# Token mixing with one folded product of the query and key weights, and a number per key added in the gating

## What is computed

```python
def token_mixing(x, d_gamma, Wq, bq, Wk, bk, Wv, bv, Wo, bo, a):
    q, k, v = x @ Wq + bq, x @ Wk + bk, x @ Wv + bv
    scores = einsum('btd,bsd->bts', q, k)                 # no softmax
    retained = einsum('bts,bsd->btd', d_gamma * scores, v)
    y = retained @ Wo + bo
    return where(y >= 0, y, a * y)
h = token_mixing(x, ...)
h = h + attn(layernorm(h))      # encoder and decoder LSTMs, 1024 steps each
h = h + ffn(layernorm(h))       # 8 experts, 2 chosen per token
```

## Time and profile before

| | us |
|---|---|
| median of 3 runs | 3925.51 (3924.63 to 3928.59) |
| the profiled execution | 3921.38 |
| its span, first to last instruction | 3919.6 |
| TensorE busy in the span | 3750.3 (96%) |
| VectorE busy | 3139.5 (80%) |
| ScalarE busy | 2391.9 (61%) |
| Pool busy | 85.4 (2%) |
| mean granted TensorE clock | 0.986 |

### The profile page before, as it was taken

How to read it: one execution, slowest core, us unless ns; L and a number is a source line. 1 busy time by engine, 2 the same in 40 slices (tenths; PEclk the granted TensorE clock), 3 DMA queues, 4 the chain that set the end, 5 groups by cost and what they waited for, 6 DMA issues and landing times. The chain is left out here.

```text
span 3919.6 us, 159989 instructions
## 1 busy us (share of the span) xinstructions
PE 3750.3 (96%) x61932; PEld 2749.2 (70%) x61932; DVE 3139.5 (80%) x21227; ACT 2391.9 (61%) x11882; POOL 85.4 (2%) x129
## 2 busy tenths in 40 slices
PE   7899999999999999999999899999999999999998
PEld 3333888888888888888888666666666666666664
DVE  6999899999999999999998677766777667776675
ACT  3232898888889889888887344444444443444443
POOL 6100000000000000000000000000000000000000
PEclk8999999999999999999999999999999999999999
DMA  3111000000000000000000000000000000000000
GB/s 91 22 25 23 3 3 3 3 3 3 3 3 3 3 3 3 3 3 3 3 3 4 4 8 8 8 6 6 8 8 8 6 7 7 8 8 6 6 8 7
DMA packets 49571, 34.01 MB, mean 9 GB/s; under 512 B 37661, under 2 KB 46877, under 8 KB 48806
## 3 DMA queue, kind: packets, MB, share of 16 engines
q1 hardware_dynamic: 48806, 23.77, 2.3%
HBM read 15.37 MB, written 8.39 MB: 6 GB/s over the span
## 5 line engine op out<-in xcount | busy, mean ns | idle before, releaser
L740 PE MATMUL bank<-xs,ident 128*128 128x128 f16 x15583 | 1415.1, 223 | 0.0
L740 PEld LDWEIGHTS bank<-xs,ident 128*128 128x128 f16 x15583 | 1010.2, 102 | 252.2 <-issue 229.8
L760 ACT ACTIVATE ifg_cell_dec<-bank 128x48 f32<-128x48 f32 x1024 | 215.2, 210 | 641.3 <-PE bank L752 641.3
L752 PE MATMUL bank<-enc_lo,u_hi 128*128 128x16 f16 x8192 | 530.1, 173 | 0.3 <-DVE enc_lo L812 0.3
L749 PE MATMUL bank<-enc_hi,u_lo 128*128 128x16 f16 x8192 | 527.8, 173 | 0.0
L775 DVE SCALAR_TENSOR_TENSOR terms_dec<-ifg_cell_dec 128x32 f32<-128x32 f32 x1024 | 197.1, 193 | 398.3 <-ACT ifg_cell_dec L760 387.2
L749 PE MATMUL bank<-enc_hi,u_hi 128*128 128x16 f16 x8192 | 501.6, 170 | 0.0
L749 PEld LDWEIGHTS bank<-enc_hi,u_lo 128*128 128x128 f16 x8192 | 338.4, 96 | 205.6 <-DVE enc_hi L806 171.2
L767 ACT ACTIVATE bank<-twice_cell_dec 128x16 f32<-128x16 f32 x1024 | 191.7, 187 | 402.4 <-DVE twice_cell_dec L781 402.4
L752 PEld LDWEIGHTS bank<-enc_lo,u_hi 128*128 128x128 f16 x8192 | 339.3, 96 | 67.9 <-DVE enc_lo L812 0.4
L749 PE MATMUL bank<-ring_hi,u_lo 128*128 128x16 f16 x4096 | 260.7, 172 | 102.3 <-DVE ring_hi L806 96.0
(11 more groups left out here) (268 smaller groups left out, 7900.8 us busy)
## 6 DMA issues: line engine op xcount, KB each, us to landing
g_rows<-tok_d_gamma_batched_dram SPq DMA_DIRECT2D x8, 512.0 KB, 6.5
x_rows<-in_x_dram SPq DMA_DIRECT2D x16, 256.0 KB, 3.0
kept_h<-tok_ln_h SPq DMA_DIRECT2D x32, 128.0 KB, 2.1
res<-kept_h SPq DMA_DIRECT2D x32, 128.0 KB
out_dram<-sums SPq DMA_DIRECT2D x32, 128.0 KB
raw_wd<-in_L_attn_Wd_dram SPq DMA_DIRECT2D x2, 256.0 KB
raw_experts<-in_L_ffn_W_dram SPq DMA_DIRECT2D x2, 256.0 KB
raw_u<-in_L_attn_Uf_dram SPq DMA_DIRECT2D x1, 256.0 KB
```

The source lines that it names most:

```text
L740: nc.tensor.matmul(spare, m.ident16[:], m.xs[:, 0, :, :].rearrange("p b t -> p (b t)"), start=False, stop=True, skip_group_check=True)
L752: last = nc.tensor.matmul(z[k], m.u_hi[c.d][:, g, :], h_lo, start=False, stop=True, skip_group_check=True)
L760: nc.scalar.activation(c.ifg_cell[:, 0:3, :], ifg, ACT.Tanh, scale=1.0 / Z_SCALE).then_inc(c.s_t_ifg, 1)
```

## The change

The scores of a batch are x M x^T plus terms with one bias, where M = Wq Wk^T. Setup makes M, Wk bq, Wq bk and bq . bk on TensorE and ScalarE. Per batch the kernel computes `k_full` = M' x for 1024 keys (two tiles, no bias matmul; ScalarE adds a bias per partition), splits it into `k_hi` and `k_lo`, and scores are k_hi and k_lo (stationary) times `xT` (moving), which is therefore double-buffered. The part that depends on the key alone comes out of the value matmuls as a 65th column; ScalarE copies it into `d_col`. The gate adds it and multiplies by gamma. The low halves are subtractions in SBUF, on VectorE for batches 0 to 4 (t = 10 and 12), on Pool for batches 5 to 15.

```diff
 # setup, SP
-                for raw, w in zip(raw_qk, (a["L0_tok_Wq"], a["L0_tok_Wk"])):
-                    for k in range(2):
-                        load(raw[k * D:(k + 1) * D, :], w)
+                load(wq[:], a["L0_tok_Wq"])
+                load(wk[:], a["L0_tok_Wk"])
+                load(wq_bq[:, D:DV], a["L0_tok_bq"][:, None])
+                load(bk[:], a["L0_tok_bk"][:, None])
...
-                for k, name in enumerate(("bq", "bq", "bk", "bk")):
-                    load(raw_mix[:, k * D:(k + 1) * D], a["L0_tok_" + name][None, :].broadcast_to([3, D]), s_b, n_b)
 # setup, TensorE (ScalarE copies each result: 4 turned weights, raw_k, two columns, raw_wvo, raw_mix)
-                nc.tensor.transpose(m.bank[4][0:D, 0:D], wv[:], m.ident[0:D, 0:D]).then_inc(s_v, 1)
+                for n, w in enumerate((wv, wq, wk)):
+                    last = nc.tensor.transpose(m.bank[4][0:D, n * D:(n + 1) * D], w[:], m.ident[0:D, 0:D])
+                last.then_inc(s_v, 1)
...
+                mm(m.bank[7][:, 0:DV], wkT[:].rearrange(twice), wq_bq[:], start=True, stop=True)
+                mm(m.bank[7][:, DV:DV + 1], wqT[:].rearrange(twice), bk[:], start=True, stop=True).then_inc(s_v, 1)
...
+        PE_TILE = {7: 0, 9: 1}
+        DVE_TILE = {10: 0, 12: 1}
+        POOL_FROM = 5
...
 # Pool, behind split_weights
+                for b in range(POOL_FROM, B):
+                    for half in range(2):
+                        cols = slice(half * HALF, (half + 1) * HALF)
+                        pool.wait_ge(s_hi, 2 * b + half + 1)
+                        nc.gpsimd.tensor_tensor(k_lo[b % 2][:, cols], k_full[half][:], k_hi[b % 2][:, cols], ALU.subtract
+                                                ).then_inc(s_lo_pool, 1)
 # TensorE, scores
-                    for q, stop in ((q_hi, False), (q_lo, True)):
-                        last = mm(z, k_both[k][:, s * P:(s + 1) * P], q[k][:, half * HALF:(half + 1) * HALF],
+                    for keys, stop in ((k_hi, False), (k_lo, True)):
+                        last = mm(z, keys[k][:, s * P:(s + 1) * P], xT[k][:, half * HALF:(half + 1) * HALF],
                                   start=not stop, stop=stop)
 # TensorE, prep t == 5: two banks, 65 columns
-                            z = bank[6][:, c * D:(c + 1) * D]
+                            z = bank[6 - c // 4][:, c % 4 * DV:(c % 4 + 1) * DV]
 # TensorE, prep, tiles
+                        pe.wait_ge(s_vk, 2 * b + half + 1)
+                        z = bank[6 - half][:]
-                        mm(z, bias, m.ones_s[:], start=True, stop=False)
-                        mm(z, w_hi[:].rearrange("p two d -> p (two d)"), x, start=False, stop=False)
-                        mm(z, w_lo[:].rearrange("p two d -> p (two d)"), x, start=False, stop=True).then_inc(s_tile, 1)
+                        mm(z, m.wk_hi[:].rearrange("p two d -> p (two d)"), x, start=True, stop=False)
+                        mm(z, m.wk_lo[:].rearrange("p two d -> p (two d)"), x, start=False, stop=True).then_inc(s_tile, 1)
 # ScalarE, prep t == 5 and tiles
+                        for half in range(2):
+                            act.wait_ge(s_vo, 2 * b + half + 1)
+                            z = m.bank[6 - half][:, 0:4 * DV].rearrange("p (c d) -> p c d", d=DV)
+                            S.copy(d_col[k][:, 4 * half:4 * half + 4].unsqueeze(2), z[:, :, D:DV])
+                            S.activation(vo[k][:, 4 * half:4 * half + 4, :], z[:, :, 0:D], ACT.Identity,
+                                         scale=MIX_SCALE ** -4).then_inc(s_vk, 1)
...
+                        if b:
+                            wait_low(act, b - 1, half)
+                        z = m.bank[6 - half][:]
+                        S.activation(k_full[half][:], z, ACT.Identity, bias=m.k_col[:, 0:1], scale=1.0 / MIX_SCALE)
+                        S.activation(k_hi[k][:, half * HALF:(half + 1) * HALF], z, ACT.Identity, bias=m.k_col[:, 0:1],
                                      scale=1.0 / MIX_SCALE).then_inc(s_hi, 1)
 # VectorE, gate and low halves
-                    TT(gated[:, n % G_RING, :], m.bank[n % Z_RING][:], m.gT[:, s, half * HALF:(half + 1) * HALF], ALU.mult
-                       ).then_inc(s_g, 1)
+                    STT(gated[:, n % G_RING, :], m.bank[n % Z_RING][:], d_col[b % 2][:, s:s + 1],
+                        m.gT[:, s, half * HALF:(half + 1) * HALF], ALU.add, ALU.mult).then_inc(s_g, 1)
...
-                        STT(low, z, 1.0 / MIX_SCALE, high, ALU.mult, ALU.subtract).then_inc(s_lo, 1)
+                        TT(k_lo[k][:, cols], k_full[half][:], k_hi[k][:, cols], ALU.subtract).then_inc(s_lo, 1)
```

More of the change, by code:

```diff
@@ L38 @@
 BIAS_MIX = 12 * H + D + E
-NBIAS = BIAS_MIX + 5 * D
+DV = D + 1
+NBIAS = BIAS_MIX + DV
 BIG = 2.0 ** 100
@@ L121, in build @@
         m.gate_bias = m.bias[:, 12 * H + D:12 * H + D + E]
-        m.q_bias, m.k_bias = (m.bias[:, BIAS_MIX + k * 2 * D:BIAS_MIX + (k + 1) * 2 * D] for k in range(2))
-        m.vo_bias = m.bias[:, BIAS_MIX + 4 * D:]
+        m.vo_bias = m.bias[:, BIAS_MIX:]
         m.ones3 = sb("ones3", [P, P], BF16)
-        m.ones_s = sb("ones_s", [P, HALF], BF16)
+        m.ones_s = sb("ones_s", [P, P], BF16)
+        m.k_col = sb("k_col", [P, 1], F32)
         m.a_col = sb("a_col", [P, 1], F32)
@@ L167, in setup @@
     with ctx:
[L168 to L171, removed]
+        raw_mix = sb("raw_mix", [3, DV], F32)
+        part = sb("part", [3, 3, DV], BF16)
+        left = sb("left", [3, 3, DV], F32)
+        wq, wk = (sb(n, [D, D], F32) for n in ("wq", "wk"))
+        bk = sb("bk", [D, 1], F32)
+        bk3 = sb("bk3", [D, 3], F32)
+        wqT = sb("wqT", [D, 2, D], F32)
+        wq_bq = sb("wq_turned_bq", [D, DV], F32)
+        wkT = sb("wkT", [D, 2, D], F32)
+        raw_k = sb("raw_k", [P, D], F32)
         wv = sb("wv", [D, D], F32)
@@ L388, in token_mixing @@
         x_split = sb("x_split", [P, NB, 2 * D], F16)
-        xT = sb("xT", [P, T], F16)
-        q_hi = [sb(f"q_hi{k}", [P, T], F16) for k in range(2)]
-        q_lo = [sb(f"q_lo{k}", [P, T], F16) for k in range(2)]
-        k_both = [sb(f"k_both{k}", [P, T], F16) for k in range(2)]
+        xT = [sb(f"xT{k}", [P, T], F16) for k in range(2)]
+        k_hi = [sb(f"k_hi{k}", [P, T], F16) for k in range(2)]
+        k_lo = [sb(f"k_lo{k}", [P, T], F16) for k in range(2)]
+        k_full = [sb(f"k_full{k}", [P, HALF], F32) for k in range(2)]
+        d_col = [sb(f"d_col{k}", [P, NB], F32) for k in range(2)]
         vo = [sb(f"vo{k}", [P, NB, D], F32) for k in range(2)]
@@ L693, in prep @@
                             ).then_inc(s_xs, 1)
-                    if t in DVE_TILE:
-                        n = DVE_TILE[t]
-                        which, half = QK_TILES[n]
+                    if t in DVE_TILE and b < POOL_FROM:
+                        half = DVE_TILE[t]
                         cols = slice(half * HALF, (half + 1) * HALF)
-                        dve.wait_ge(s_hi, 4 * b + n + 1)
-                        if which == "q":
-                            low, high, z = q_lo[k][:, cols], q_hi[k][:, cols], m.bank[5 + n % 2][:]
-                        else:
-                            low = high = k_both[k][D:2 * D, cols]
-                            z = m.bank[5 + n % 2][D:2 * D, :]
-                        STT(low, z, 1.0 / MIX_SCALE, high, ALU.mult, ALU.subtract).then_inc(s_lo, 1)
+                        dve.wait_ge(s_hi, 2 * b + half + 1)
+                        TT(k_lo[k][:, cols], k_full[half][:], k_hi[k][:, cols], ALU.subtract).then_inc(s_lo, 1)
                 for t in range(NT):
```

105 lines of the change are left out of this document (53 added, 52 removed).

## The result

The changed kernel takes 3916.1 us as a median of ten runs (3912.0 to 3919.0). The kernel before, ten runs with the three shown above among them, takes 3926.4 (3919.4 to 3934.7). The ratio is 0.9973, with a 95% interval of 0.9963 to 0.9983, so the change saves 10.3 us, give or take some four. The prediction was 3916.1.

What follows compares the result with a forecast made beforehand. TensorE was taken to bound a steady batch. Setup and the long interval -4.5, one interval -0.5, eleven steady ones -4.9 and the last +0.5 gave -9.4 us: 3912 profiled, 3916.1 us as a median, range 3903 to 3925.

Steps and rivals of the forecast that it cites:

- The floor: TensorE's time for a steady mixing batch: 20.45 less 1.72 us of dropped matmuls, 18.73 us.
- the sum: Total for the mixing: -4.5 to the long interval's end, -0.5, -4.9 in eleven steady intervals, +0.5 at the last; -9.4 us.
- the 1.3 us: TensorE's expected standing time per steady batch, waiting for gates and the LN split, making the period 20.0 us.
- VectorE's own lag: From L644 to the products behind the LN transposes, VectorE alone with eight dearer gates delays TensorE 0.6 us a batch.
- B: Rival: Pool and VectorE miss each other and the number per partition is free; period 18.9, 3903.5 us; chance 0.15.
- C: Rival: gates cost 0.07 more but Pool's work falls beside gates; period 19.3 to 19.4, 3909 us; chance 0.12.
- D: Rival: Pool also holds L682 or L686, or batch 3's k_lo costs another Pool instruction; 3922.5 to 3926.5 us; chance 0.20.
- E: Rival: Pool's subtraction is longer than 1.16 us, each extra microsecond adding one to the period; up to 3938 us; chance 0.06.
- F: Rival: the new gate is streamed at half rate because of its number per partition; 78 us more, 4004 us; chance 0.02.
- SP's last issue ends setup now, so 1.3 us earlier: Setup: without raw_mix loads SP's issues end 1.3 us sooner, so Pool's split and x come 1.3 us earlier.
- my bound: Limit on the change at the long interval's end, taken as -4.5 us with bounds of -1 and -7.
- one instruction further: Case behind the -7 us bound: VectorE is one instruction further when Pool's long instructions end.

Runs made afterwards that it cites:

- e3: Changed kernel, but the gate takes the constant 0.0 instead of the number per key, leaving the key's term out; 3907.4 us.
- e11: Changed kernel with TensorE making the two key tiles at gates 6 and 12 and VectorE's turns at 13 and 15; 3902.0 us.
- e5: Changed kernel with the second key tile made at t = 13 instead of 9 and VectorE's turns at 13 and 15; 3911.0 us.
- e7: Changed kernel with Pool's second subtraction made twice, the first time into a tile nobody reads; 3921.4 us.
- e8: Changed kernel without the two column loads bq and bk, Pool filling their tiles with zeros; 3914.3 us.
- e1: Changed kernel with all low halves of the keys left on VectorE and none on Pool; 3911.2 us.
- e2: Changed kernel with Pool subtracting 8 instead of 512 columns in each half from batch 5 on, all waits kept; 3896.9 us.
- e9: Changed kernel with Pool's bias rows of the later stages made in eight pieces of 201 columns; 3909.4 us.

## Why the prediction was right, and where it was not

**The steady batch: right in its cause and its size.** The floor was 18.73, and 18.78 was measured with both causes out. (A pair of products with its four score matmuls takes 1.98 us, 0.11 more than 1.01 and 4 x 0.215: each pair has a small gap, in both kernels, so the floor holds.) Period 20.0, measured 19.95; the eleven intervals gave -5.2 us for the -4.9 of the sum. L713 held: 0.71 for my 0.6 to 0.8. Gate 0.746 for 0.75. Pool's subtraction 1.16 for 1.16, 22 of them. The interval with VectorE's k_lo came to 19.80 for 19.9, the last one +0.43 for +0.5.

**The composition of the 1.3 us: wrong in its form.** I added 0.6 for VectorE's own lag and 0.6 to 0.7 for Pool. The table shows a hold that shrinks by what VectorE is late. What sets both holds is Pool's first subtraction. It starts 8.28 us behind yT in after and 8.27 in e3, behind the k_hi of the first tile. It holds L700 to its end, and through L700, ScalarE's square root and k_hi it sets the second one, which starts 10.94 and 10.93 us behind yT. Dearer or cheaper gates don't move either, they only change how long VectorE stands. The sum came out (0.05 + 0.42 + 0.75 = 1.22) because I had taken L713's stand from 238.1, 9.5 us behind L644, and that is the arrival of a VectorE that already has the dearer gates: from L677 (the old L644) to L713 it is 9.58 us in after, 9.39 with Pool's 8 columns and 8.97 with both out. The mis-sized terms are Pool's first subtraction, 0.21 at L700 for my "0.1 at most" (0.50 with cheaper gates), and the gates, 0.42 for 0.53. What would have misled a reader: a faster gate, which my sum prices at half a microsecond a batch, is worth 0.01 here.

Which of VectorE's instructions are held is a thing that the page "SBUF — State Buffer" of the Trainium skill states (section "SBUF: two separate sides"): the port that both engines share goes to one of them for a whole instruction, and VectorE asks for it when it has two SBUF inputs or runs in a mode that uses two ports. The traces agree: the reduction at 225.49 (0.68) and the gates ran beside Pool, L713 with its two SBUF inputs did not. L700 has one input and was held too; that it ran in such a mode no run here shows.

**Rivals.** B, Pool and VectorE miss each other and the number is free, is 18.78 in the table, and no kernel with its whole work had it. C, the number costs but Pool falls beside gates, is just what e11 built: 19.20. I had priced it at 19.3 to 19.4. D did not come: L713 stood until Pool's end, L715 and L719 were free. Its second half, batch 3's k_lo behind one more Pool instruction, came in e5 and e11. E had a microsecond of Pool's time at a microsecond of period; e7 measured 0.91 for 1.11. F, half rate, did not show: 746 ns.

**Setup: wrong.** I had SP done 1.3 us earlier and the first gate at 37. SP issues as many loads as I counted, but two of them stretched. SP's queue in after, then Wf's halves in the first trace of before and the experts' bias in the second:

```profile
12.48 2.42 SPq L198 DMA_DIRECT2D raw_w<-in_L_attn_Wf_dram  x2
...
21.02 2.78 SPq L198 DMA_DIRECT2D b<-in_L_ffn_b_dram  x1
...
27.94 5.02 SPq L462 DMA_DIRECT2D x_rows<-in_x_dram  x3
```

```profile
13.73 1.11 SPq L191 DMA_DIRECT2D raw_w<-in_L_attn_Wf_dram  x2
```

```profile
20.89 1.08 SPq L191 DMA_DIRECT2D b<-in_L_ffn_b_dram  x1
```

The issue of Wf's halves took 1.3 us more than in the earlier trace rows's execution, which used up the head start: it ended at 14.90, for 14.84 before. The experts' bias took 1.7 more; x's load left 1.6 us later than before, not 1.3 earlier; the first gate stands at 40.38. The part of the step behind SP was right: from x's load to the first gate it was 14.4 us and is 12.4, and I had counted 2.2 for it. The failed term is "SP's last issue ends setup now, so 1.3 us earlier": I priced each issue by its duration in before, as if it were the same in another row of loads. The bias's issue was long in all twelve traces with the changed setup; that of Wf's halves scattered from 1.11 to 3.09 us among them. What makes the two issues longer stays open; that the column loads alone do is excluded by e8.

**The long interval: a compensating error.** Predicted 120 for its end, -4.5; measured 117.44, -7.1 (-6.2 against the second trace of before), which is my bound. In e1, e2 and e7, whose code is the same up to there, it ends at 117.0 to 118.1, so this is no scatter. Pool was not 1.3 to 2 us earlier but 5 later: its bias table starts at 84.76 for 80.93, 1.35 of that because its first instruction waits for SP's last load, the rest because instructions of its own were stretched (0.97 us for 0.53, 0.75 for 0.43), which I put down to VectorE. Yet VectorE was further when it mattered:

```profile
106.05 3.75 DVE L719 TENSOR_TENSOR tok_ln_split<-tok_ln_square,tok_ln_split 128x512 f16<-128x512 f32 x1
109.72 0.68 DVE L731 TENSOR_TENSOR k_lo<-k_full,k_hi 128x512 f16<-128x512 f32 x1
...
114.47 0.68 DVE L725 SCALAR_TENSOR_TENSOR x_split<-x_rows,x_split 128x512 f16<-128x512 f32 x1
```

```profile
105.69 3.56 POOL L345 TENSOR_TENSOR bias_left<-bias_left 3x1608 f32<-3x1608 f32 x1
109.35 5.17 POOL L346 TENSOR_SCALAR bias_left<-bias_part,ident 3x1608 f32<-3x1608 bf16 x1
114.61 4.01 POOL L347 TENSOR_TENSOR bias<-bias_left 3x1608 bf16<-3x1608 f32 x1
```

Before, Pool's last long instruction (110.15 to 113.73) held L682. In after the last hold is that of L719, the layernorm's last, by the instruction which ends at 109.25; the two long ones behind it hold nothing: k_lo (109.72) gets in at the start of the first and x_split (114.47) just ahead of the second. That is the "one instruction further" of my lower bound. So the last hold ends 4.5 us earlier, for my 1.3 to 2, and from there to yT it is 8.2 us for 10.8: 2.6 less, for my 2.5. The mis-sized term is the first. That long instructions are the cause is shown by e9, where pieces took the interval to 20.28 us.

**The total.** Predicted for the mixing -9.4, measured -12.5 (-11.6 against the second trace of before); for the median -9.4, measured -10.3 with some 4 us to either side. That the forecast of 3916.1 was hit to a tenth is luck: the median of before moved by 0.9 us with more runs, and the error in the long interval lies inside the scatter of the later stages.

## What to carry to other kernels

An engine that is idle is not a free place for work: ask which instructions of the other engines its work holds, and put it beside others (here 0.75 us a batch by moving two tiles and their low halves by one to three steps, with not one instruction removed). Long instructions on such an engine hold the other one for their whole length, so cut them into pieces, and check what then ends later. Where two delays meet at one instruction, measure them two by two: a hold that ends at a fixed time takes up the other delay, and a saving ahead of it is worth nothing. Where an engine waits once a batch, look on which side of the wait its work stands: here two matmuls in front of it cost nothing, and moving them behind it took back 0.43 us of the 0.55 that e5 had gained.

## What the runs showed of the hardware that I had not expected

- A number per partition in VectorE's SCALAR_TENSOR_TENSOR costs 0.06 us over a constant, for 512 columns from PSUM (746 and 685 ns).
- The hold goes both ways: Pool's own short subtractions of the weights, 0.43 us in the earlier trace rows, took 0.75 in places after the change, and one bias instruction of 4.34 us took 5.17 when L719 and k_lo of VectorE stood around its start.
- An SP issue isn't of a fixed length: 1.04 and 1.08 us in both traces of before, 2.69 to 4.45 in twelve of the changed setup, for the same load.
- The granted clock can fall in the middle of a steady stretch and cost 1.6 us of one batch (e7: down to 0.50 from 279 to 281 us, after TensorE had been busy for 0.51 of 2 us).
- The later stages, with the same code, scatter by 13 us over 14 traces.
